# Attentions of a 12-layer decoder kernel: the late products and X's turning issued ahead of a round's values on TensorE

## What is computed

```python
for l in range(4):                                  # 8 heads of 64
    h = rmsnorm(x, sg[l])
    x = attn_block(h, h, sWq[l], sWk[l], sWv[l], sWo[l], ..., mask) + x        # self attention, 512 keys
    h = rmsnorm(x, cg[l])
    x = attn_block(h, ctx, cWq[l], cWk[l], cWv[l], cWo[l], ..., None) + x      # cross attention, 154 keys
    h = rmsnorm(x, fg[l])
    x = gelu(h @ fW1[l] + fb1[l]) @ fW2[l] + fb2[l] + x

def attn_block(...):
    q, k, v = xq @ Wq, ctx @ Wk, ctx @ Wv           # q and k get rotary positions
    a = softmax(q k^T)
    return (a v) @ Wo + bo
```

## Time and profile before

| | |
|---|---|
| median of 3 runs | 4173.82 us (4170.47 to 4176.15) |
| profiled execution | 4180.67 us |
| its span, first to last instruction | 4179.0 us |
| PE / DVE / ACT / POOL busy, share of the span | 93% / 66% / 47% / 23% |
| mean granted clock of TensorE, share of full speed | 0.977 |

### The profile page before, as it was taken

The page is one execution under the profiler, slowest core; times in us unless marked ns, Lnnn a source line. Parts: engine busy times, 40 slices in busy tenths (PEclk is TensorE's granted clock), DMA queues, the critical chain, the costliest instruction groups (busy, mean ns, idle before and its releaser), DMA issues. The chain is left out here.

```text
span 4179.0 us, 70765 instructions
## 1 busy us (share of the span) xinstructions
PE 3893.9 (93%) x23508; PEld 2394.3 (57%) x23508; DVE 2766.9 (66%) x8036; ACT 1978.4 (47%) x5740; POOL 948.6 (23%) x1040
## 2 busy tenths in 40 slices
PE   7999899999999999999989998999999999999998
PEld 4644455665655655666646444565556556555665
DVE  3787767677767747664447886776777776476644
ACT  1732445655555533663228224555565555346722
POOL 0145332233322200000001462322323321000000
PEclk8999999999999999999979999999999999999999
DMA  1100000000000010000010000000000000201000
GB/s 57 43 17 1 17 7 18 24 17 24 17 24 2 26 58 21 31 37 9 4 59 6 17 1 17 7 17 24 18 24 17 24 2 26 72 7 56 12 9 11
DMA packets 15853, 91.87 MB, mean 22 GB/s; under 512 B 2176, under 2 KB 8064, under 8 KB 12032
## 3 DMA queue, kind: packets, MB, share of 16 engines
q1 hardware_dynamic: 15488, 87.27, 5.8%
HBM read 86.22 MB, written 1.05 MB: 21 GB/s over the span
## 5 line engine op out<-in xcount | busy, mean ns | idle before, releaser
L610 PE MATMUL ps_O<-wide,V 128*64 128x256 f32 (+4 forms) x5152 | 596.2, 393 | 1.9 <-ACT wide L638 1.9
L691 ACT ACTIVATE EX<-NB,neg 128x154 f32<-128x154 f32 (+3 forms) x768 | 402.7, 531 | 107.6 <-DVE neg L719 107.6
L561 PE MATMUL ps_S<-KT,QT 64*128 64x154 f32 (+7 forms) x1936 | 373.5, 456 | 59.9 <-POOL QT L1619 25.3
L656 POOL COPY RX<-recips 128x256 f32<-128x256 f32 (+2 forms) x356 | 156.6, 440 | 1127.9 <-DVE recips L734 1127.9
L745 DVE TENSOR_TENSOR QT<-ps_O,RS 128x512 f32<-128x512 f32 x212 | 146.5, 691 | 395.2 <-PE ps_O L610 394.6
L640 DVE COPY wide<-ps_P 128x512 f32<-128x512 f32 (+4 forms) x528 | 339.8, 647 | 75.2 <-PE ps_P L592 72.4
L610 PEld LDWEIGHTS ps_O<-wide,V 128*64 128x64 f32 (+4 forms) x5152 | 266.8, 127 | 194.6 <-issue 110.7
L429 POOL TENSOR_TENSOR small<-small 128x4 f32<-128x4 f32 x112 | 113.6, 1014 | 1065.6 <-DVE small L414 902.8
L561 PE MATMUL ps_T<-KT,QT 64*128 64x154 f32 (+5 forms) x968 | 322.2, 435 | 3.4 <-ACT EX L691 3.4
L561 PE MATMUL ps_OUT<-KT,QT 64*128 64x154 f32 (+5 forms) x968 | 325.2, 434 | 0.1
L592 PE MATMUL ps_P<-consts,EX 128*128 128x128 f32 (+1 forms) x1956 | 294.1, 286 | 25.9 <-ACT RS L647 13.0
(11 more groups left out here) (388 smaller groups left out, 8231.5 us busy)
## 6 DMA issues: line engine op xcount, KB each, us to landing
weights<-in_w_dram SPq DMA_DIRECT2D x10, 1664.0 KB, 6.9
weights<-in_w_dram SPq DMA_DIRECT2D x2, 6148.0 KB, 17.5
weights<-in_w5next_dram SPq DMA_DIRECT2D x6, 1664.0 KB, 6.9
weights<-in_w_dram SPq DMA_DIRECT2D x2, 4200.0 KB, 12.9
weights<-in_reltab_dram SPq DMA_DIRECT2D x2, 4096.0 KB, 14.1
weights<-in_w_dram SPq DMA_DIRECT2D x8, 640.0 KB, 3.9
weights<-in_w_dram SPq DMA_DIRECT2D x5, 832.0 KB, 4.5
weights<-in_w_dram SPq DMA_DIRECT2D x2, 2050.0 KB, 7.9
```

The costliest lines, as they stand in the source:

```text
L561: ins = pe.matmul(S4[k][:, a * N:(a + 1) * N], QT[strip, c, qts[a] * P:(qts[a] + 1) * P], self.keys(c)[strip, 0:N], start=True, stop=True)
L610: ins = pe.matmul(O1[self.slot * j:self.slot * (j + 1), q0 * P:(q0 + self.nq) * P], self.value(c * self.hpc + j, kc), self.probs(rd, j)[:, ...
L656: pool.tensor_copy(RX[:, q0 * P:(q0 + self.nq) * P].rearrange("p (n s) -> p n s", s=self.slot), of.unsqueeze(2).broadcast_to([P, self.nq * ...
L691: ins = act.activation(ex[:, a * N:(a + 1) * N], src, ACT.Exp, bias=neg[:, at:at + 1], scale=-1.0 if self.added else 1.0, accum_out=sums[: ...
```

## The change

In PE's list the late work of step `i` moves from behind the values of round `i-2` to ahead of them, directly behind the turnings of round `i-1`. The instructions, their counts, the slots in the ring and all waits stay; the other engines' lists stay as they are.

```diff
@@ -592,6 +592,10 @@
                                     ins = pe.transpose(self.banks[s % nb][0:self.kc, b * P:(b + 1) * P],
                                                        ex[:, a * N + kc * self.kc:a * N + (kc + 1) * self.kc], ident)
                             ins.then_inc(r.probsT, 1)
+                    for j in self.late.get(i, ()):
+                        if self.late_at[j] >= nb:
+                            self.evacuated(pe, r, self.late_at[j] - nb)
+                        late(pe, j)
                     rd = i - 2
                     if wo is not None and i == self.steps - 1:
                         self.project(pe, r, wo, 0, self.chunks - 2)
@@ -611,10 +615,6 @@
                                                 self.value(c * self.hpc + j, kc), self.probs(rd, j)[:, kc, :],
                                                 start=(kc == 0), stop=(kc == last))
                         ins.then_inc(r.av, 1)
-                    for j in self.late.get(i, ()):
-                        if self.late_at[j] >= nb:
-                            self.evacuated(pe, r, self.late_at[j] - nb)
-                        late(pe, j)
                     if beside:
                         beside(i)
```

## The result

The changed kernel takes 4229.74 us (median of 4 runs, 4226.3 to 4236.82) against 4173.32 us before (4 runs): 56.4 us slower, a ratio of 1.0137 with a 95% interval of 1.0123 to 1.0152. The forecast was 4226 us (4204 to 4244), slower with 89%.

What follows compares the result with a forecast made beforehand. PE was taken as the bound behind the change, so exposed waits are kept: 27.4 + 8.8 + 14.1 + 1.6 = 51.9 us on the profiled 4180.67, 4232.6, less 6.85 for the median: 4226 us (4204 to 4244).

Steps and rivals of the forecast that it cites:

- Where PE is the bound: From step 3 of a self attention to its last projection, PE works 42.10 of 42.10 us, so no idle time absorbs delay.
- Rival C: Waits are taken up by PE's gap at the next attention's start: no change, 4174 us, +-8; chance 7%.
- Rival B: DVE truly bounds steps 3 to 5; its idle time before rotations comes back, so 4140 us; chance 4%.
- Rival A: Each wait in step 2 of a self attention brings the clock down: 27 us more, 4253 us; chance 5%.
- Self attention, step 2: Product 5 and X's turning wait for DVE's copies, no longer covered by the values: +1.71 us each, 27.4 us in all.
- Step 3: Self attentions: product 6 does not wait, PE loses nothing, give or take 0.1 us; DVE gets 0.5 us later.
- Step 4: Self attentions: product 7 waits for DVE's later copy of k=1: +0.55 us each (-0.1 to +0.8), 8.8 us in all.
- Cross attention: Step 2: X's turning waits for DVE's copy of k=1: +0.88 us each (0.8 to 1.0), 14.1 us in all.
- L3 and L0: X's turning at step 3: L3's attention 0.4 us each, 1.6 in all; L0's cross attention 0.
- the idle time ended by L640: Sign in the profile after: PE idle time released by DVE's copies grows by some 35 to 45 us in all.
- The clock: Few drops expected from the new waits in self attentions; a phase shift may add or remove some, +-5 us.

## Why the prediction was right

**Where PE is the bound.** The reading of the earlier trace rows held: what was lost in steps 2 to 4 stayed lost, 0.00 us in all later steps and in the gaps between attentions. Rival C fell by these zeros. Rival B fell as well: counted from the step's first turning, the rotation of product 5 did start earlier (4.71 us in place of 5.11), and DVE only waited longer for scores; that of product 6 started later, behind the multiplication. Rival A fell by the clock at 1.00 and by step 2's cost, 1.83 to 1.84 in all 16.

**Self attention, step 2.** Forecast +1.71, measured +1.84. The wait for k=1's copy was exact (start 0.05 us after its end). X's turning started 0.15 us after the copy of k=2 (1026.09 - 1025.94) and not 0.05, and was followed by the values after 0.56 in place of 0.53. 16 x 0.13 = 2 us of the sum.

**Step 3.** No wait, as said; the 0.1 us that I set aside as a bound is there, -0.11.

**Step 4.** Forecast +0.55, measured +0.73 at this step and +0.62 together with step 3's gain. The chain (values later, multiplication later, rotation later, copy later, product 7 waits) was right in each link, and the two runs with one product each show it. DVE was 0.61 us later by it where I took 0.5: the rotation starts 0.73 after the scores (1036.43 - 1035.70), before 0.12. The rest is product 7, which kept PE for 1.06 us where I took 1.0.

**Cross attention.** Forecast +0.88, measured +0.92. Here too X's turning started 0.15 us after the copy and not 0.05 (1199.50 - 1199.35); some of these 0.1 us came back, as the values follow X's turning after 0.56 us, where the scores followed it after 0.59.

**L3 and L0.** Forecast 1.6 and 0, measured 0.4 and 0.4; by the moved steps and the ones behind them alone, 0.65 and 0.0. In L3 more was given back by the wait for ScalarE's copy than the half I took: 0.46 of 0.62 us on the mean of the four.

**Sum.** 51.9 us forecast, 56.4 measured. By the steps, self attention's step 2 is 2.0 us above its term, steps 3 and 4 together 1.2, the cross attentions 1.5 (with the clock in it), and L3 and L0 are 0.8 below. No term was far off, and no large errors cancelled, so the sum is not luck. One of the signs that I named for the profile after was off: I wrote that the idle time ended by L640 would grow by 35 to 45 us. It grew by 53. By the steps' own waits (1.5, 0.25, 0.6 and 0.9 us, 16 times each) it should have read 52, so this was a slip against my own sum.

**The clock.** With waits of 1.40 and 0.17 us in step 2 and 0.66 in step 4 of every self attention, the granted clock stayed at 1.00. It does fall in some cross attentions, before the change as after it. The Trainium skill, "TensorE: Matmul & The Clock Gate", section "A second HAM failure mode: psum-queue depth-cycling", tells of a kernel in which short idle spells of PE between groups of matmuls that cycle through banks made the clock oscillate. By that rule the time would have come nearer to rival A's; at these places the trace does not bear it out.

## What to carry to other kernels

Ahead of moving a piece of work forward on a bound engine, look up for which buffer it waits and who frees it, and measure the time from its new place to that moment; the work that it is moved past may be what covers the wait. Where the bound engine has no idle time behind, as here, such an exposed wait is paid in full, and handing work earlier to an engine that is not the bound bought nothing. And an instruction that is taken earlier in an in-order queue can idle that queue for its input: two copies moved forward on DVE, at 66% busy, cost 13 us until they were left alone in step 1, where what stands behind them in the queue is soon needed by PE. In step 3 the same idle time of DVE cost nothing.

## What was not expected of the hardware

One and the same move costs the same to 0.01 us at step 2 of all 16 self attentions, where the clock is full. What spreads is the clock. The same cross attention shows between +0.6 and +1.24 us for one and the same change, by whether a stretch of 3.4 us at the lower level falls into its step 1 before or after. What PE did ahead of such a stretch need not differ: at the start of the cross attention of the earlier trace rows it idled 0.96, 0.53, 0.62 and 0.22 us, and the clock fell; at the start of that of the earlier trace rows it idled 0.96, 0.53, 0.62 and 0.21 us, and the clock stayed at 1.00. And the opening stretch up to the first turnings took 133.8 us in one execution and 125.4 in another, at a mean granted clock of 0.85 and 0.91.

```profile
0.00:133.80 133.80, 103.59 (x402) 65.89 (x402) 59.74 (x190) 32.43 (x61) 9.31 (x20) 0.85 0.22 77
```

```profile
0.00:125.40 125.40, 94.81 (x402) 59.55 (x402) 59.70 (x190) 32.47 (x61) 9.33 (x20) 0.91 0.23 82
```

The first is the kernel before, the second the kernel after. So two profiled executions alone would have put the change at 50.5 us; step by step they give 56.1.
